# The last attention batch of a one-core transformer block: a router's exponential, its weights and a weight's cast take other places in the engines' queues

## The reference, cut to what matters

```
x = x + attention(layernorm(x))      # 32 heads of 16, causal, with ALiBi bias, then a projection
x = x + ffn(layernorm(x))            # router and experts, below
x = x + mlp(layernorm(x))            # silu(gate) with the smaller half set to 0, times up, then down
x = x + ffn(layernorm(x))            # the same experts again

def ffn(h):
    ratio = mean|h| over the last tokens / (mean|h| over the first 30% + 1e-8)        # one a batch
    scores = softmax([h, ratio] @ gate_w + gate_b)                                    # 3 experts
    top_val, top_idx = top_k(scores, 2); top_val /= sum(top_val) + 1e-8
    act = [tanh, gelu, silu](h @ w1[e] + b1[e]);  expert[e] = act @ w2[e] + b2[e]
    return sum over i in (0, 1) of top_val[..., i] * expert[top_idx[:, 0, i]]         # experts by the first token
```

## Time and profile before

| | |
|---|---|
| timed runs | 684.03, 683.9 and 686.13 us, median 684.03 |
| profiled execution | 683.48 us, span of the core 681.7 us |
| mean granted TensorE clock | 0.997 of full speed |
| busy: PE, weight loads, DVE, ACT, POOL | 643.5 (94%), 489.6 (72%), 483.5 (71%), 343.5 (50%), 92.2 us (14%) |
| chain that ended last | PE 77%, DVE 13%, ACT 4% |
| last batch, from its first Exp to the first expert product | 217.4 to 240.8 us |

### The profile page before, as it was taken

The page is one execution under the profiler, slowest core; times in us unless marked ns, Lnnn a source line. Parts: engine busy times, 40 slices in busy tenths (PEclk is TensorE's granted clock), DMA queues, the critical chain, the costliest instruction groups (busy, mean ns, idle before and its releaser), DMA issues.

```text
span 681.7 us, 10305 instructions
## 1 busy us (share of the span) xinstructions
PE 643.5 (94%) x3848; PEld 489.6 (72%) x3848; DVE 483.5 (71%) x921; ACT 343.5 (50%) x539; POOL 92.2 (14%) x185
## 2 busy tenths in 40 slices
PE   4888999999998899999999899999999999999997
PEld 4866678679676577887788676766857665787876
DVE  6755585796589789877697666375374898788555
ACT  5313644613633763532388997476483915434221
POOL 4411002102100120101142010100100250000000
PEclk9989999999999999999999999999999999999999
DMA  8395513322744222000062000000003206000000
GB/s 281 104 258 184 156 32 97 117 70 74 239 134 149 109 88 79 0 1 1 24 224 86 1 0 0 1 1 0 1 0 101 86 0 231 2 32 16 16 31 32
DMA packets 31908, 52.15 MB, mean 76 GB/s; under 512 B 3449, under 2 KB 17148, under 8 KB 30303
## 3 DMA queue, kind: packets, MB, share of 16 engines
q1 hardware_dynamic: 31282, 49.84, 22.5%
q10 hardware_dynamic: 576, 1.64, 1.0%
HBM read 42.87 MB, written 8.40 MB: 75 GB/s over the span
## 4 chain that ended last, share of the span: by engine, by line
PE 77%; DVE 13%; ACT 4%; issue 1%; DMA 1%; ACTq 1%; POOL 1%; SPq 0%; DVEq 0%; POOLq 0%
PE ps L2023 14%; PE ps L1892 13%; PE ps L1859 13%; PE ps L2092 10%; PE ps L1722 5%; DVE nmax L1100 3%; PE ps L1800 2%; PE ps L1738 2%; PE ps L1868 2%; PE ps L1702 2%; DVE nmax L1097 2%; PE ps L1790 2%; ACT sign_junk L989 1%; PE ps L2081 1%; ACTq L508 1%
## 5 line engine op out<-in xcount | busy, mean ns | idle before, releaser
L2092 PE MATMUL ps<-wdT,prodT 128*128 128x512 f32 (+1 forms) x176 | 76.9, 592 | 0.0
L817 ACT ACTIVATE probsT<-ps 128x1536 f32<-128x1536 f32 x32 | 46.2, 1450 | 28.2 <-PE ps L1790 28.0
L2092 PEld LDWEIGHTS ps<-wdT,prodT 128*128 128x128 f32 (+1 forms) x176 | 32.8, 190 | 38.3 <-issue 38.3
L859 ACT ACTIVATE funs<-ps 128x512 f32<-128x512 f32 x16 | 9.5, 596 | 92.3 <-PE ps L1861 80.5
L683 POOL TENSOR_SCALAR ln_spread<-ln_moments 128x1 f32<-128x1 f32 x24 | 7.5, 311 | 273.7 <-DVE ln_moments L1171 273.6
L1625 DVE COPY prodT<-ps 128x512 f32<-128x512 f32 (+1 forms) x24 | 13.7, 599 | 41.3 <-PE ps L2081 41.0
L1177 DVE SCALAR_TENSOR_TENSOR junk<-x_sb,gate_row 128x512 f32<-128x512 f32 x48 | 41.1, 857 | 1.0
L1440 DVE SCALAR_TENSOR_TENSOR x_sb<-b_row,coef,x_sb 128x512 f32<-128x512 f32 x48 | 38.0, 792 | 1.8
L1100 DVE TENSOR_REDUCE nmax<-ps 128x4 f32<-128x1024 f32 x32 | 38.8, 1212 | 0.0
L989 ACT ACTIVATE sign_junk<-mlp_size_next,minus_guess 128x1376 bf16<-128x1376 f32 x24 | 34.6, 1443 | 0.8
L989 ACT ACTIVATE sign_junk<-mlp_size_main,minus_guess 128x1376 bf16<-128x1376 f32 x24 | 34.6, 1442 | 0.7
(11 more groups left out here) (302 smaller groups left out, 1730.8 us busy)
## 6 DMA issues: line engine op xcount, KB each, us to landing
cuts<-parts SPq DMA_DIRECT2D x16, 384.0 KB, 2.8
qst<-cuts SPq DMA_DIRECT2D x48, 128.0 KB, 2.6
w_first_raw<-in_L_ffn_w SPq DMA_DIRECT2D x6, 1024.0 KB, 7.8
w_second_raw<-in_L_ffn_w SPq DMA_DIRECT2D x6, 1024.0 KB, 8.7
kst<-cuts SPq DMA_DIRECT2D x36, 128.0 KB, 2.7
wqkv_raw<-in_L_attn_a_w_attn SPq DMA_DIRECT2D x3, 1024.0 KB, 7.9
wdT<-in_L_attn_b_w_down SPq DMA_DIRECT2D x1, 2560.0 KB, 10.0
wg_raw<-in_L_attn_b_w_gate SPq DMA_DIRECT2D x1, 2048.0 KB, 8.3
```

The source lines that it names most:

```text
L817: nc.scalar.activation(probsT[:, g % 2, :].rearrange("p (k n) -> p k n", k=3), slot[g % 2], ACT.Exp).then_inc(exp_ok.sem, 1)
L2092: last = nc.tensor.matmul(ps[:, Y_BANK, :], prodT[0:m, c, :], wdT[0:m, c, :], start=(c == 0), stop=(c == IC - 1))
```

## The change

In the last batch's loop ScalarE takes the router's Exp behind group 5's Exp instead of group 3's. The cast of expert 2's second matrix leaves the loop and stands behind the copies of the last turned heads, directly ahead of the first expert's Tanh. On VectorE `ranks` moves from group 3's turn to group 4's, and the logit row from 4's to 3's. `weights` is cut into `tops` (the top two shares, in group 5's turn) and `shares` (spread over the experts, in group 6's turn ahead of `middle_weights`). The other three routers (`route1`'s second group and both of `route2`) call `weights`, which now calls both, so their instructions stay as they were.

```
                     nc.scalar.activation(probsT[:, g % 2, :].rearrange("p (k n) -> p k n", k=3), slot[g % 2],
                                          ACT.Exp).then_inc(exp_ok.sem, 1)
-                    if b == B - 1 and g == 3:
+                    if b == B - 1 and g == 5:
                         route_exp(route1.groups[0], *GROUPS[0])
-                    if b == B - 1 and g == 4:
-                        second_weights(w2_first, 0, FIRST_W2[:1])
                     if b >= 1 and g == 5:
                         magnitudes(norm2, route1, (b - 1) * TB)
...
+            second_weights(w2_first, 0, FIRST_W2[:1])
             functions(ffn1, 0, 0)
             normal_row(norm2, 2, ffn1.row)
...
                         if g == 2:
                             router.scores()
-                        elif g == 3:
+                        elif g in (3, 7):
+                            logit_row(route1, (b - 1) * TB, (g - 3) // 4)
+                        elif g == 4:
                             router.ranks()
-                        elif g in (4, 7):
-                            logit_row(route1, (b - 1) * TB, (g - 4) // 3)
                         elif g == 5:
-                            router.weights()
+                            router.tops()
                         elif g == 6:
+                            router.shares()
                             router.middle_weights()
...
                 def weights(self):
+                    self.tops()
+                    self.shares()
+
+                def tops(self):
...
                     link(nc.vector.reciprocal(inverse, part))
                     link(tt(top, top, inverse.unsqueeze(1).broadcast_to([P, 2, nt]), ALU.mult))
+
+                def shares(self):
+                    nb, nt, t0, t1, link, post = self.nb, self.nt, self.t0, self.t1, self.link, self.post
+                    tt = nc.vector.tensor_tensor
+                    top = self.row(15, 2 * nt).rearrange("p (s t) -> p s t", s=2)
                     shares = [coef[:, t0:t1, :].rearrange("p (b j) e -> p b j e", b=nb), self.tiles(16)]
                     for s in range(2):
                         for j in range(TB):
                             (post if j < TB - 1 else link)(
                                 tt(shares[s][:, :, j, :], top[:, s, j::TB].unsqueeze(2).broadcast_to([P, nb, E]),
                                    self.has[:, s, :, :], ALU.mult))
```

## The result

The changed kernel took 682.11 us (median of 10 runs, 681.5 to 684.02) against 684.74 us (10 runs, 683.55 to 686.13): ratio 0.9967, 95% interval 0.9957 to 0.9978, so 1.5 to 2.9 us less. Its profiled execution took 681.57 us, span 679.8, against 683.48 and 681.7. Timed again later (12 runs, median 683.62, against 21 runs of the kernel before, median 684.08), the ratio was 0.9982 (0.9969 to 0.9995), 0.3 to 2.1 us less. The ratios are estimates over all runs and not quotients of the medians, which are 0.9962 and 0.9993.

A forecast was written before the change was run, and what follows sets the result against it. In the last attention batch TensorE was held to wait for late ScalarE probabilities, and at the end for VectorE. 0.59 + 0.88 + 0.30 - 0.06 = 1.71 us off 684.03 gives 682.3 us, range 681.2 to 683.6.

The forecast's parts named there:

- Group 4's turn: Last batch's loop: with the router's Exp moved, TensorE's turn falls from 2.84 to 2.25 us, 0.59 us gained.
- Group 5's turn: Last batch's loop: with the cast moved out, TensorE's turn falls from 3.13 to 2.25 us, 0.88 us gained.
- The step to group 7: Loop's end: with tops inside its VectorE turn, the step from group 6's product falls from 2.15 to 1.85 us, 0.30 gained.
- VectorE's longer group 6 turn: Shares and middle weights keep VectorE busy 1.91 us, while group 7's copy could begin after 1.85: 0.06 us lost.
- The rule on VectorE's small instructions: Skill page: the next VectorE operation awaits an empty pipe, semaphores cost nothing extra; group 6's eight instructions then take 1.28 us.
- The cast at no cost: Ahead of the first Tanh: ScalarE idles 3.35 us, so the 1.89 us cast fits with 1.46 us left, cost 0.
- only a cast of more than 10 us: Ahead of the Tanh: only that or a hidden wait makes the kernel slower, by 2 us or more.
- The tail: Rival, loop's end: VectorE is late, group 7's step stays 2.15 us; gain only 1.2 us, 682.8 us; chance 0.14.
- the turns did stay at 2.25 us: Rival, groups 6 and 7: fuller ScalarE and TensorE lengthen turns, the Exps' delay returns; half the gain, 683.2 us; chance 0.08.
- nothing was slower: Rival, experts' start: the moved cast holds up the experts, costing 2 us or more, 686 us; chance 0.05 including the unseen.
- within 0.3%: Whole time: chance 0.64 that the change stays under 0.3% (2.05 us), the least a measurement can tell from no change.

The follow-up runs named there:

- e1: The kernel before with only the router's Exp moved behind group 5's Exp; from group 0's product to the turned heads 18.82 us, 1.15 less.
- e2: The kernel before with only expert 2's cast moved ahead of the first Tanh; from group 0's product to the turned heads 19.07 us, 0.90 less.
- e3: The changed kernel with both ScalarE moves undone, VectorE's new order kept; group 0's product to the turned heads 19.72 us, 0.25 less than the kernel before.
- e4: The kernel before with both ScalarE moves, VectorE's order unchanged; group 0's product to the turned heads 18.48 us, 0.21 more than the changed kernel.
- e6: The changed kernel with the moved cast done six times in its place; first expert product to the end 447.48 us, 6.5 more.
- e10: The changed kernel with the moved cast done five times in its place; first expert product to the end 3.0 us longer.
- e9: The changed kernel with group 7's logit row behind the loop and TensorE's turn back of group 7 between the two row turns; ratio to the kernel before 0.9963, later 0.9967.
- e8: The changed kernel with group 7's logit row taken behind the loop; group 0's product to the turned heads 18.12 us, 0.15 less.

## Why the prediction was right

The forecast was 1.71 us off, made of four terms, and the ruler shows 1.70.

- *Group 4's turn, 0.59.* Measured 0.58 (2.84 to 2.26), in e1 0.59. Right.
- *Group 5's turn, 0.88.* Measured 0.88, in e2 0.88. Right for both moves together; e1 shows that 0.54 of it comes back with the Exp's move alone, so the two terms can't be given to the two edits one by one.
- *The step to group 7, 0.30.* Measured 0.23: 1.92 us instead of the 1.85 of the earlier trace rows. The mechanism was right (e3 has it, e4 lacks it), the size was off. The copy of group 6 begins 1.00 us behind its product, and not 0.92, with VectorE idle before it. The 1.91 or 1.92 stands in every execution with tops in that turn. In groups 4 and 5 the copy follows a piece that doesn't end in a wait for its own result, and comes at 0.92 and 0.93; tops ends in one. Whether that is the cause wasn't tried.
- *VectorE's longer group 6 turn, -0.06.* It is VectorE that sets the last copy, as predicted, and it costs 234.85 - 233.90 - 0.92 = 0.03. The four terms as measured sum to 0.58 + 0.88 + 0.23 - 0.03 = 1.66. The other 0.04 of the 1.70 are hundredths in steps for which nothing was forecast, so that 1.71 and 1.70 agree to 0.01 is luck: two faults of 0.07 and 0.03, of opposite sign, and those hundredths.
- *The rule on VectorE's small instructions.* Taken as the prediction took it, it gave 1.28 us for the eight instructions, the rows 1.11; they took 1.09. The same section of the Trainium skill's page "VectorE: DVE Perf Modes" adds that a next operation which isn't held back starts earlier, and the prediction left that out. On the semaphore the rows disagree with it for instructions as small as these. In `ranks` the second one waits for nothing, the third for the second:

```profile
229.19 0.15 DVE L1317 TENSOR_TENSOR tiny<-tiny 128x4 f32<-128x4 f32 x1
229.26 0.15 DVE L1318 TENSOR_TENSOR tiny<-tiny 128x2 f32<-128x2 f32 x1
229.45 0.16 DVE L1320 SCALAR_TENSOR_TENSOR tiny<-tiny 128x2 f32<-128x2 f32 x1
```

  One begins 0.07 us behind the other without a wait and 0.19 with one, so here a wait isn't free.
- *The cast at no cost.* Right: the Tanh waits 1.55 us behind it where 1.46 were counted. The bound on this edit is 5.8 us by e6 and e10; the prediction counted 1.46 + 2.8 + 2.2 = 6.5. Its place was wrong, since the addition behind the first mix is late before the turned rows are, and so was its price: past it I let each microsecond count once; the clock made 3.5 us of waiting into 6.5 in e6, and a second wait made 1.6 into 3.0 in e10. So "only a cast of more than 10 us" was wrong too: with 9.7 us of casts in that place, e10 is already 1.4 us slower than the kernel before from group 0's product to the end (18.26 + 444.03 against 19.97 + 440.89, and nearly the same between).
- *The rivals.* The tail kept its gain; the turns did stay at 2.25 us, though in group 5's ScalarE was full (group 6's Exp at 229.84 has no idle time ahead of it); nothing was slower.
- *The time.* Forecast 682.3, measured 682.11 and, the second time, 683.62. That the first came so close is luck in part: its medians differ by 2.63 us and not by 1.71, but the median before was 684.74 where the forecast had started from 684.03. The second lies at the upper end of the range that was given, 683.6, with medians only 0.46 us apart. The chances, 0.64 for "within 0.3%" and 0.32 for more, were fair: the first ratio says 0.33%, the second 0.18%, the ruler 0.25%.

## What to carry to other kernels

Look for the instruction on a support engine that waits in the middle of a regular loop, and move its reader and itself to where its input is ready anyway; a delay of the loop's own instruction counts only beyond its slack, and two delays in one queue share that slack, so sum them in the new order. In a chain that ends a stage, taking work off one engine pays only up to the next engine's order (0.15 us of 0.78 here), and the edit that frees the rest may be one of order alone (0.44 us more in e9). For a difference of a few tenths of a percent, measure from one event of the stage to another in the profile, not the whole time.

## What the runs showed of the hardware

The scatter of the timed runs, 2.5 us and more for one kernel, goes for the most part with the mean clock that TensorE was granted. Of the 21 later runs of the kernel before, the eleven at 0.997 took 683.42 to 684.08 us, the six at 0.995 684.46 to 685.98, the three at 0.993 685.95 to 686.67; one at 0.998 took 684.90. The changed kernel's three runs at 0.997 beside them took 681.78 to 682.03, so at that clock the two kernels stand clear of each other; its eight at 0.995 took 682.72 to 685.61 and overlap with the other's. The loss can lie in stretches that no edit touched. Group 0's product starts between 218.73 and 219.97 us, and the executions differ in the clock early on. Stretches of 30 to 40 and 40 to 60 us in the kernel before, the changed one and e8:

```profile
30.00:40.00 10.00, 8.27 (x51) 7.57 (x50) 3.17 (x5) 0.28 (x1) 0.76 (x1) 0.83 1.06 262
40.00:60.00 20.00, 15.56 (x136) 12.42 (x135) 17.12 (x26) 3.62 (x9) 2.31 (x2) 1.00 0.89 262
```
```profile
30.00:40.00 10.00, 7.42 (x58) 6.65 (x56) 3.18 (x5) 0.63 (x2) 0.42 (x1) 1.00 1.04 257
40.00:60.00 20.00, 14.54 (x127) 11.61 (x128) 17.30 (x26) 3.41 (x9) 2.30 (x2) 1.00 0.88 260
```
```profile
30.00:40.00 10.00, 7.46 (x58) 6.66 (x56) 3.17 (x5) 0.56 (x2) 0.49 (x1) 1.00 1.04 256
40.00:60.00 20.00, 15.96 (x117) 11.88 (x118) 16.61 (x24) 2.95 (x7) 2.31 (x2) 0.83 0.90 262
```

The second had full clock in both and started group 0 first, at 218.73; the first started it at 219.03, the third at 219.95. All three executions with full clock in both stretches started it by 219.07, and the two with less than full clock in both at 219.96 and 219.97. Where only one was short, it began anywhere from 218.91 to 219.95, so the clock of these stretches isn't all of it. The same kernel can also lose it much later. e9 in its two executions, 500 to 545 us:

```profile
500.00:545.00 45.00, 43.26 (x181) 29.73 (x180) 29.78 (x63) 31.05 (x51) 8.16 (x11) 1.00 0.20 71
```
```profile
500.00:545.00 45.00, 43.22 (x177) 30.20 (x176) 28.12 (x65) 30.26 (x50) 6.15 (x11) 0.96 0.20 71
```

The second of them needs 442.56 us for the rest instead of 440.98, 1.6 us more, without a new wait. What lowers the clock there wasn't tried.
